# Layer 1's attention weights of rows 0 to 511 in two key halves, s_i on VectorE, and a one-instruction leaky rectifier

## The reference

```python
Xw = X @ Wv + bv
sj = Xw @ aw[:d, 0]
si = Xw @ aw[d:, 0]
e = leaky_relu(sj[:, None, :] + si[:, :, None] + ab[0], negative_slope=0.2)
alpha_matrix = A * exp(e)
transition = alpha_matrix / (sum(alpha_matrix, axis=-1) + 1e-12)
for k in range(3):
    H = H + Xk @ Wk[k] + bk[k]
    Xk = transition @ Xk
return relu(H)
```

## Time and profile before

| | us |
|---|---|
| median of three runs | 3239.82 (3238.65 to 3240.64) |
| profiled execution, its own time | 3240.96 |
| its span, first to last instruction | 3239.2 |
| TensorE busy, matmuls | 3078.7 (95%) |
| VectorE busy | 2119.0 (65%) |
| ScalarE busy | 1710.0 (53%) |
| mean granted clock of TensorE | 0.982 |

### The profile page before, as it was taken

One profiled execution on the slowest core, in us unless ns is written; L12 is line 12 of the kernel. 1 busy time (PEld: TensorE's weight loads), 2 busy tenths in 40 slices (PEclk: granted clock), 3 DMA queues, 4 the chain that ended last, 5 costly groups with the idle time before them and its releaser, 6 DMA issues.

```text
span 3239.2 us, 71078 instructions
## 1 busy us (share of the span) xinstructions
PE 3078.7 (95%) x28440; PEld 2706.9 (84%) x28440; DVE 2119.0 (65%) x3844; ACT 1710.0 (53%) x2945; POOL 444.6 (14%) x1666
## 2 busy tenths in 40 slices
PE   7999999999999998999989999899998999989999
PEld 6988789887898788987789877898778987789877
DVE  5636976279762797627966279663886538875388
ACT  3425854258442684426844268442784327743277
POOL 0001210012100121001211012111121111211112
PEclk9999999999999999999999999999999999989999
DMA  5022131121311213212133021330213302133020
GB/s 211 26 80 63 48 141 48 58 69 44 138 59 50 66 51 131 79 33 67 47 131 98 16 70 43 129 105 12 68 51 121 105 14 68 53 117 105 17 47 19
DMA packets 145270, 234.51 MB, mean 72 GB/s; under 512 B 12840, under 2 KB 113965, under 8 KB 144941
## 3 DMA queue, kind: packets, MB, share of 16 engines
q1 hardware_dynamic: 144940, 229.96, 22.0%
HBM read 120.86 MB, written 83.89 MB: 63 GB/s over the span
## 4 chain that ended last, share of the span: by engine, by line
PE 84%; DVE 10%; ACT 3%; issue 1%; SPq 1%; POOL 1%; DMA 0%; DVEq 0%; POOLq 0%; ACTq 0%
PE ps L463 15%; PE ps L465 15%; PE ps L464 15%; PE ps L661 14%; PE ps L651 9%; PE ps L679 7%; DVE rsum L1172 2%; PE ps L543 2%; PE ps L597 1%; PE ps L518 1%; DVE xt_lo L1093 1%; PE ps L532 1%; PE ps L692 1%; SPq L366 1%; DVE al_area L1206 1%
## 5 line engine op out<-in xcount | busy, mean ns | idle before, releaser
L1328 DVE CUSTOM_DVE_ANT_0 r<-ps,adjn 128x1024 f32<-128x1024 f32 x512 | 620.7, 1212 | 20.9 <-DVE xr L1364 11.3
L1037 ACT ACTIVATE r<-r,nmax 128x1024 f32<-128x1024 f32 x512 | 585.3, 1143 | 23.7 <-POOL nmax L455 22.6
L463 PE MATMUL ps<-u_hi,t_hi 128*128 128x256 f32 x2048 | 590.3, 288 | 5.3 <-DVE u_lo L1086 4.8
L464 PE MATMUL ps<-u_lo,t_hi 128*128 128x256 f32 x2048 | 581.5, 284 | 0.0
L465 PE MATMUL ps<-u_hi,t_lo 128*128 128x256 f32 x2048 | 581.2, 284 | 0.0
L661 PEld LDWEIGHTS ps<-ident,r 128*128 128x128 f32 x4096 | 461.5, 140 | 116.1 <-issue 77.6
L661 PE MATMUL ps<-ident,r 128*128 128x128 f32 x4096 | 537.0, 274 | 7.4 <-DVE pt L1344 7.2
L1344 DVE COPY pt<-ps 128x512 f32<-128x512 f32 x512 | 353.0, 689 | 93.1 <-PE ps L661 71.3
L463 PEld LDWEIGHTS ps<-u_hi,t_hi 128*128 128x128 f32 x2048 | 394.3, 193 | 9.8 <-DVE u_lo L1086 6.4
L836 ACT ACTIVATE pt<-ps 128x512 f32<-128x512 f32 x512 | 304.2, 594 | 176.0 <-PE ps L661 157.7
L464 PEld LDWEIGHTS ps<-u_lo,t_hi 128*128 128x128 f32 x2048 | 395.0, 193 | 0.0
(11 more groups left out here) (157 smaller groups left out, 5282.4 us busy)
## 6 DMA issues: line engine op xcount, KB each, us to landing
adjn<-in_adj SPq DMA_DIRECT2D x64, 512.0 KB, 3.5
t_spill<-t_hi SPq DMA_DIRECT2D x64, 512.0 KB, 4.1
t_spill<-t_lo SPq DMA_DIRECT2D x64, 512.0 KB, 5.1
t_hi<-t_spill SPq DMA_DIRECT2D x32, 1024.0 KB, 5.3
t_lo<-t_spill SPq DMA_DIRECT2D x32, 1024.0 KB, 8.2
xn<-in_x SPq DMA_DIRECT2D x16, 512.0 KB, 4.6
x_spill<-xn SPq DMA_DIRECT2D x64, 128.0 KB, 1.7
q_stack<-u_hi SPq DMA_DIRECT2D x64, 128.0 KB, 2.4
```

Source lines behind the costliest of these rows:

```text
L463: pe.matmul(dst, a_hi, b_hi, start=first, stop=False, skip_group_check=check)
L464: pe.matmul(dst, a_hi, b_lo, start=False, stop=False, skip_group_check=check)
L1037: act.activation(r[:, s % RSLOTS, :], r[:, s % RSLOTS, :], ACT.Exp, bias=nmax[:, s % 4:s % 4 + 1], accum_out=prow[:, qt % 2, h:h + 1]).the ...
L1328: dve.tensor_tensor_reduce(out=r[:, s % RSLOTS, :], in0=ps[:, 2 * (s % 2):2 * (s % 2) + 2, :].rearrange("p a c -> p (a c)"), in1=adjn[:, q ...
```

## The change

Four edits, all in layer 1 of each element.

1. The weights of row tiles 0 to 3 are made in two parts: part 0 over keys 0 to 511, part 1 over keys 512 to 1023; tiles 4 to 7 remain whole (part 2). The order of the twelve blocks is `AL`. Each part has its own transposes (four in one bank), its own copies, and its own half of the hop: twelve matmuls accumulate into the tile's place, twelve more later. Each tile has a place of its own (`hop_place`) in the four ACC banks, and the first two row products of the second hop use the banks 4 and 5.
2. s_i: TensorE's `si_columns` goes. VectorE multiplies the normalised row tile with a row `wsi_row` that is the same on all partitions, and sums, 256 wide (`s_i`), for tile t - 2 behind the statistics of tile t, and for tiles 6 and 7 in layer 1's order. `wsi_row` is made once in the setup by two matmuls and a copy.
3. leaky_relu is one ScalarE instruction, `Prelu` with a slope of 0.2 and s_i as the bias column; `scaled` and `linear` go, and `si_scaled` with them.
4. The order of all three engines in layer 1 is written anew, below. The row sums of part 0 go to `rsum_a` and are added to those of part 1.

```diff
+    AL = [(0, t) for t in range(TPH)] + [(1, t) for t in range(TPH)] + [(2, t) for t in range(TPH, NT)]
-            return ((6, 7), (4, 5))[unit[1] % 2]
+            return ((6, 7), (4, 5))[unit[2] % 2] if unit[1] == 2 else (4 + unit[2] % 2,)
-                [("sj", 0), ("si", 0), ("v", 0), ("v", 1), ("sj", 1)] + [("v", k) for k in range(2, PAIRS)] + [("si", 1)] +
+                [("sj", 0), ("v", 0), ("v", 1), ("sj", 1), ("v", 2), ("v", 3)] +
...
+                pe.matmul(ps[:, ACC + 3, 0:F], st_aw[:, dt, 1:2].broadcast_to([P, P]), st_wvt[:, dt, :],
+                          start=(dt == 0), stop=(dt == FT - 1))
...
+            def hop(b, part, t):
+                pe.wait_ge(tp_free, nth(b, TP_UNITS, tp["al", part, t] + 1))
+                for j in range(NT)[al_keys(part)]:
+                    if part < 2 and t == 0:
+                        rows_wait(b, "v", j)
+                    last = three(hop_place(t), t_hi[:, j, t * P:(t + 1) * P], t_lo[:, j, t * P:(t + 1) * P],
+                                 uh[:, j, :], ul[:, j, :], j == 0, j == NT - 1)
...
+                s_j(b, 0)
+                project_pairs(b, "v", W_K2, xt_wait(b, 1), range(2))
+                transpose_x_half(b, 1, 1)
+                transpose_alpha(b, 0, 0)
+                transpose_alpha(b, 0, 1)
+                s_j(b, 1)
+                hop(b, 0, 0)
+                transpose_alpha(b, 0, 2)
+                hop(b, 0, 1)
+                transpose_alpha(b, 0, 3)
+                project_pairs(b, "v", W_K2, xt_wait(b, 1), range(2, 3))
+                hop(b, 0, 2)
+                project_pairs(b, "v", W_K2, xt_wait(b, 1), range(3, 4))
+                hop(b, 0, 3)
+                transpose_alpha(b, 1, 0)
+                transpose_alpha(b, 1, 1)
+                hop(b, 1, 0)
+                transpose_alpha(b, 1, 2)
+                hop(b, 1, 1)
+                transpose_alpha(b, 1, 3)
+                hop(b, 1, 2)
+                transpose_alpha(b, 2, 4)
+                hop(b, 1, 3)
+                for t in range(TPH, NT):
+                    if t + 1 < NT:
+                        transpose_alpha(b, 2, t + 1)
+                    else:
+                        project_pairs(b, "z", W_K1, xt_wait(b, 1), range(2))
+                    last = hop(b, 2, t)
...
+                    act.activation(al(part, t), row, ACT.Prelu, bias=si_col[:, t:t + 1], scale=1.0,
+                                   alpha=SLOPE).then_inc(e_lin, 1)
...
                 normalise(b, 0, NT - 2)
+                leaky(0, 0)
+                normalise(b, 0, NT - 1)
+                exponential(0, 0)
                 rows_from_pr(b, "v", range(1))
+                leaky_exp(0, 1)
+                x_transposed(b, 1, 1)
                 rows_from_pr(b, "v", range(1, 2))
+                act.wait_ge(t_out, nth(b, 32 * NT, 32 * NT))
+                al_transposed(0, 0)
+                leaky_exp(0, 2)
+                al_transposed(0, 1)
+                leaky_exp(0, 3)
+                al_transposed(0, 2)
+                leaky_exp(1, 0)
+                rows_from_pr(b, "v", range(2, 3))
+                al_transposed(0, 3)
+                leaky_exp(1, 1)
+                rows_from_pr(b, "v", range(3, PAIRS))
+                al_transposed(1, 0)
+                leaky_exp(1, 2)
+                al_transposed(1, 1)
+                leaky_exp(1, 3)
+                al_transposed(1, 2)
+                leaky_exp(2, 4)
+                al_transposed(1, 3)
+                leaky_exp(2, 5)
+                for t in range(TPH, NT):
+                    al_transposed(2, t)
                     if t + 2 < NT:
+                        leaky_exp(2, t + 2)
...
+            def s_i(b, t):
+                dve.wait_ge(ln_done, nth(b, LN_PER, t + 1))
+                alone()
+                dve.tensor_tensor_reduce(out=y[:, t % 4, :], in0=xn[:, t, :], in1=wsi_row[:, :], scale=1.0, scalar=0.0,
+                                         op0=ALU.mult, op1=ALU.add, accum_out=si_col[:, t:t + 1]).then_inc(si_done, 1)
...
+                s_j(0)
+                s_i(b, NT - 2)
+                weights(0, 0)
+                rows_from_pr(b, "v", U_V, range(1))
+                s_i(b, NT - 1)
+                weights(0, 1)
+                x_transposed(b, 1, 1)
+                rows_from_pr(b, "v", U_V, range(1, 2))
+                al_transposed(0, 0)
+                s_j(1)
+                weights(0, 2)
+                al_transposed(0, 1)
+                weights(0, 3)
+                al_transposed(0, 2)
+                weights(1, 0)
                 rows_from_pr(b, "v", U_V, range(2, 3))
+                al_transposed(0, 3)
+                weights(1, 1)
                 rows_from_pr(b, "v", U_V, range(3, PAIRS))
+                al_transposed(1, 0)
+                weights(1, 2)
+                al_transposed(1, 1)
+                weights(1, 3)
+                al_transposed(1, 2)
+                weights(2, 4)
+                al_transposed(1, 3)
```

More of the change, by code:

```diff
@@ L222, in build_program @@
         e_lin = sem("e_lin")
-        e_scaled = sem("e_scaled")
         e_exp = sem("e_exp")
@@ L534, in transpose_adj, with transpose_alpha, s_j @@
                     last.then_inc(tp_full, 1)
[L536 to L543, removed]
-                last.then_inc(tp_full, 1)
+            def transpose_alpha(b, part, t):
+                pe.wait_ge(al_ready, nth(b, len(AL), AL.index((part, t)) + 1))
+                if part == 2 and t == TPH:
+                    pe.wait_ge(pr_free, nth(b, PR_UNITS, pr["v", PAIRS - 1] + 1))
+                tp_wait(b, tp["al", part, t])
+                for j in range(NT if part == 2 else TPH):
+                    last = pe.transpose(al_banks(part, t)[:, j, :], al(part, t)[:, j * P:(j + 1) * P], ident)
+                last.then_inc(tp_full, 1)
+            def hop(b, part, t):
[5 more added lines that the diff above has]
+                                 uh[:, j, :], ul[:, j, :], j == 0, j == NT - 1)
+                return last
+            def s_j(b, half):
+                pe.wait_ge(tp_free, nth(b, TP_UNITS, tp_x(1, half) + 2))
+                dst = pr_bank(b, pr["sj", half])
+                cols_h = slice(half * 512, (half + 1) * 512)
+                for ft in range(FT):
+                    last = three(dst, repeated(wsj_hi, ft), repeated(wsj_lo, ft), xt_hi[:, ft, cols_h],
+                                 xt_lo[:, ft, cols_h], ft == 0, ft == FT - 1)
+                last.then_inc(pr_full, 1)
             def project(dst, w, rows, a_hi=xt_hi, a_lo=xt_lo):
@@ L588, in repeated @@
                 return w[:, ft, 0:1].broadcast_to([P, P])
[L590 to L599, removed]
             def xt_wait(b, layer):
@@ L728, in _ @@
                         transpose_x_half(b, 1, 0)
[L731 to L743, removed]
@@ new lines, in exponential, with leaky_exp, al_transposed @@
+                def exponential(part, t):
+                    act.wait_ge(e_lin, nth(b, len(AL), AL.index((part, t)) + 1))
+                    act.activation(al(part, t), al(part, t), ACT.Exp).then_inc(e_exp, 1)
+                def leaky_exp(part, t):
+                    leaky(part, t)
+                    exponential(part, t)
+                def al_transposed(part, t):
+                    act.wait_ge(tp_full, nth(b, TP_UNITS, tp["al", part, t] + 1))
+                    copy(t_hi[:, al_keys(part), t * P:(t + 1) * P], al_banks(part, t)).then_inc(tp_hi, 1)
@@ new lines, in _ @@
+                weights(1, 2)
[4 more added lines that the diff above has]
+                al_transposed(1, 3)
+                for t in range(TPH, NT):
+                    if t + 1 < NT:
+                        weights(2, t + 1)
+                    al_transposed(2, t)
+                dve.wait_ge(al_ready, nth(b, len(AL), len(AL)))
+                dve.tensor_tensor(rsum[:, 0:TPH], rsum[:, 0:TPH], rsum_a[:, :], ALU.add).then_inc(sums_read, 1)
```

127 lines of the change are left out of this document (55 added, 72 removed).

## The result

The changed kernel takes 3211.7 us (median of four runs, 3209.97 to 3213.56) against 3239.8 us: a ratio of 0.9914, 95% interval 0.9896 to 0.9931, 28 us less. The forecast was 3209 with a range of 3183 to 3232. The profiled execution took 3213.6 us; its span from first to last instruction is 3211.7 us, 27.5 less than before.

What follows compares the result with a forecast made beforehand. TensorE, busy 95% of the span, was taken as the bound. 3241.0 less 57.6 (layer 1 chain) plus 2.0 (setup) plus 25 (clock) gives 3210.4, less 1.1 for the median: 3209 us, range 3183 to 3232.

Steps and rivals of the forecast that it cites:

- TensorE's work and s_i: Layer 1: 32 s_i matmuls per element leave TensorE, 3.4 us at full clock, 5.2 as they ran.
- The chain at full clock: Layer 1, s_j to hop's end in element 2: 7.2 us less per element, 57.6 for eight.
- Hole by hole: TensorE stalls in layer 1: 0.3 for sj_row, 2.4 before first weights' transposes, 1.1 before first half-hop, 0.95 at first whole tile.
- Where the hole comes from: Before the first weights' transposes: 2.4 us, because two weight tiles stand ahead of x's copies on ScalarE and VectorE.
- The price of s_i and Prelu: Layer 1: 256-wide multiply-and-sum on VectorE 0.41 us; Prelu on ScalarE 0.70 us for 512 columns, 1.14 for 1024.
- Rival D: ScalarE: Prelu is outside Exp's table, so each alternation loads one, 24 loads per element; about 3337 us; chance 0.05.
- The value of Prelu: Layer 1 weights: VectorE loses 1.19 us per tile; the value is only that the weights exist sooner.
- The clock term: Behind layer 1's 2.4 us hole: half clock in five elements of eight, 5 us each, 25 us.
- The likeliest rival, B: Layer 1: the clock falls in three to eight elements; 3199 to 3224 us; chance 0.50.
- Rival A: Layer 1: the clock stays up, at most two falls; 3184 to 3194 us, 3186 taken; chance 0.22.
- Rival C: Layer 1 half tiles: ScalarE's queue ends last, 3.6 us per element, 29 in all; 3224 to 3238 us; chance 0.18.
- Setup: Before element 0: two fp32 matmuls and a copy on TensorE's chain, 2.0 us more, once.

Runs made afterwards that it cites:

- fill: The changed kernel plus idle matmuls that nobody reads, in layer 1's 2.57 us hole and the two holes at layer 2's start; 3188.0 us, ratio 0.9838.
- order: The changed kernel with x's second-half copies ahead of tile 1's work on ScalarE and VectorE, and s_j's second half ahead of tile 1's transposes; 3189.7 us, ratio 0.9841.
- the two filled kernels: Kernel before with s_i on VectorE, whole tiles, old order, idle matmuls in layers 1 and 2: with Prelu 3201.5 us (0.9880), with old rectifier 3203.5 us (0.9870).
- si_only: The kernel before with only s_i moved to VectorE; whole tiles, Identity and add-and-max, old order; 3221.5 us, ratio 0.9937.
- before_fill: The kernel before plus idle matmuls in its 1.74 and 2.34 us layer 1 holes and at layer 2's start; 3228.8 us, ratio 0.9950.
- si_prelu: The kernel before with s_i on VectorE and Prelu for Identity and add-and-max; whole tiles, old order; 3221.3 us, ratio 0.9942.
- fill_l1: The changed kernel plus 10 idle matmuls in layer 1's 2.57 us hole only, layer 2 untouched; 3191.2 us, ratio 0.9833.

## Why the prediction was right, point by point

- *TensorE's work and s_i.* Right. The s_i edit alone gives 20 of the 28 us.
- *The chain at full clock, 7.2 us per element.* Nearly right. With the holes filled and the clock up (`fill`), the stage of element 2 runs from 874.42 to 923.83, 49.4 us, 6.5 less than before; predicted were 48.7. Its first row and the first one behind the hop:

```profile
874.42 0.40 PE L480 MATMUL ps<-xt_hi,wsj_hi 128*128 128x512 f32 x1
...
923.83 0.28 PE L480 MATMUL ps<-w_hi,xt_hi 128*128 128x256 f32 x1
```

Hole by hole: 2.4 predicted, 2.57 found; 1.1 and 0.98; 0.95 and 0.78. The first one, for sj_row, was mis-sized: 0.3 against 0.71, because two s_i instructions stand ahead of it, those of row tiles 4 and 5, where only the last was counted. The four together make 0.3 of the 0.7 us; the rest I did not follow. VectorE's queue in the changed kernel, element 2:

```profile
880.18 0.42 DVE L1202 CUSTOM_DVE_ANT_0 y<-xn,wsi_row 128x256 f32<-128x256 f32 x1
...
882.26 0.43 DVE L1202 CUSTOM_DVE_ANT_0 y<-xn,wsi_row 128x256 f32<-128x256 f32 x1
...
882.81 0.75 DVE L1255 TENSOR_SCALAR sj_row<-ps,e_const 128x512 f32<-128x512 f32 x1
```

- *Where the hole comes from.* Right, and shown by `order`.
- *The price of s_i and Prelu.* 0.42 and 0.71 us, as taken. Rival D is out: one table load in the whole run. Prelu and Exp take turns 96 times each without another load. By the Trainium skill ("ScalarE: Activation LUTs", "Table sets: the hidden batching unit") functions of one set need no load between them; the trace agrees.
- *The value of Prelu.* The prediction gave it none of its own except earlier weights. The times do not show even that; the traces of the two filled kernels show 0.5 us per element.
- *The clock term.* Its size came out, its place did not: this is the step that failed, and the sum was saved by a second error, by luck. Predicted were five falls of 5 us in layer 1, 25 us. Found were eight of 1.7, 14 us, and seven more of 1.5 at the start of layer 2, which the prediction left at full clock: together 24 us, which `fill` measures as 25. The likeliest rival, B, came true by its condition (three to eight elements fall), but with eight falls at its own price of 5 us it would have been 3224, and with eight at 1.7 us 3198. Taking the fall's length from the old one (10 us at 0.50) was wrong. Behind the new hole dense work follows and the clock is back after 3.4 us, where the old one was followed by two-column matmuls and two more waits. That this difference is the reason is not shown: in `si_only`, which has no two-column matmuls but a hole of 4.2 us, the fall lasts 7 us in seven elements and 10 in one.
- *Rival A* was the case of no falls: 3186 predicted. It did not come true in the changed kernel; once its holes are filled, 3188 is measured. *Rival C*, ScalarE as the bound, is not seen: after the holes it waits for TensorE, 2.0 us at 895.15.
- *Setup.* 2.0 predicted, 2.1 found.

## What to carry to other kernels

A hole on TensorE has two prices, its length and the slower matmuls behind it; here a hole of 2.57 us cost 1.7 us of slower work behind it, and the clock fell at another hole, in layer 2, where it had not before. When blocks are put ahead in hand-written queues, look at what stands behind them in every queue: one tile's Prelu, Exp and weights ahead of x's copies cost 24 us with the clock behind them, and halves and order together had brought 14. Where a hole cannot be closed, matmuls that do nothing can pay for themselves. They also measure the clock's share, if the trace shows that the clock then stays up; in `before_fill` it did not.

## What the runs showed of the hardware that I had not expected

- The same two holes (0.94 and 1.57 us, the same work around them) lowered the granted clock in one of eight elements before, in one of `si_only`, in seven of `si_prelu`, in eight of the changed kernel, in six of `order` and in one of `fill_l1`. A start 1.9 us later changed nothing. Without the half-clock stretch some 80 us earlier seven of the eight falls were gone in `fill_l1`; but in `order`, which has no such stretch either, the clock fell in six, and in `si_only`, which has it in all eight elements, in one. What decides it stays open. Each count is of one traced execution, and executions of one kernel can differ: the four of `si_prelu` had mean granted clocks between 0.981 and 0.987.
- Behind the hole of 2.57 us the clock was back after 3.4 us in eight of eight elements. Behind the one of 2.34 us, followed by two-column matmuls and waits, it was back after 10 us in seven and after 7 in one; behind `si_only`'s of 4.2 us after 7 in seven and 10 in one. So a hole's length alone does not decide how long the fall lasts: the one of 2.57 us had a shorter fall than the one of 2.34.
